# A gated-feature attention stage: another order of its round, TensorE's blocks in two pieces, two feature turns copied by VectorE

## What is computed

```python
def _psi(x):                                  # x: tokens x 64 of one head
    gen = x @ proj_w.T + proj_b
    A, Bg, Th = gen[..., 0:8], gen[..., 8:16], clip(gen[..., 16:24], -8, 8)
    return concat([A * exp(Th) + Bg * cos(Th), Bg * sin(Th)])
Q = Q_input @ Wq_w.T + Wq_b                   # K and V are the context itself
pq, pk = _psi(Q), _psi(K)
tensor, spinor = <two bilinear forms of pq and pk>
wedge = sqrt(max(|pq|^2 |pk|^2 - tensor**2 - spinor**2, 0) + 1e-6)
hodge = sqrt(|pq|^2 + 1e-6) * sqrt(|pk|^2 + 1e-6)
w = softmax((g0*wedge + g1*tensor + g2*spinor + g3*hodge) / 4 / temperature)
out = (w @ V) @ Wo_w.T + Wo_b
x = layernorm(x + out)
```

## Time and profile before

| | |
|---|---|
| runs of the kernel before | 2824.83, 2836.79, 2835.43 us |
| the profiled execution: its own time, its span | 2834.78 us, 2833.1 us |
| busy in the span: PE, PEld | 2371.9 us (84%), 1503.3 us (53%) |
| busy in the span: DVE, ACT, POOL | 1695.8 us (60%), 1363.7 us (48%), 325.7 us (11%) |
| mean granted TensorE clock | 0.908 of full speed |
| the psi stage, first transposes to last norm | 2006.9 to 2580.5 us of the span |

### The profile page before, as it was taken

How to read it: one execution, slowest core, us unless ns; L and a number is a source line. 1 busy time by engine, 2 the same in 40 slices (tenths; PEclk the granted TensorE clock), 3 DMA queues, 4 the chain that set the end, 5 groups by cost and what they waited for, 6 DMA issues and landing times. The chain is left out here.

```text
span 2833.1 us, 32030 instructions
## 1 busy us (share of the span) xinstructions
PE 2371.9 (84%) x11624; PEld 1503.3 (53%) x11624; DVE 1695.8 (60%) x3500; ACT 1363.7 (48%) x1968; POOL 325.7 (11%) x299
## 2 busy tenths in 40 slices
PE   6888888876888888887999699997568878777998
PEld 4656666652333333334566456565355655555886
DVE  5666666624666666654643598989566666743232
ACT  2333333311555555562222565654188888782221
POOL 0000000000000000000156400000111111100000
PEclk7999999966999999999899899998789999998999
DMA  2000000006333333214034512111200000002000
GB/s 77 8 16 15 16 16 15 8 8 165 53 68 68 61 66 57 47 27 162 16 59 65 106 38 68 45 68 46 102 8 31 30 31 30 23 15 75 15 23 23
DMA packets 104949, 132.46 MB, mean 47 GB/s; under 512 B 21748, under 2 KB 87556, under 8 KB 104792
## 3 DMA queue, kind: packets, MB, share of 16 engines
q1 hardware_dynamic: 90440, 115.58, 15.2%
q0 software_dynamic: 11904, 14.69, 3.2%
q10 hardware_dynamic: 2448, 0.14, 0.1%
HBM read 73.69 MB, written 31.20 MB: 37 GB/s over the span
## 5 line engine op out<-in xcount | busy, mean ns | idle before, releaser
L987 DVE TENSOR_REDUCE xattn_tops<-region 128x2 f32<-128x1024 f32 x256 | 306.3, 1220 | 128.9 <-PE region L771 128.8
L924 ACT ACTIVATE xattn_probs<-region 128x1024 f32<-128x1024 f32 x256 | 256.3, 1022 | 126.1 <-PE region L760 125.0
L156 PE MATMUL region<-gla_xT,weights_even 128*128 128x512 f32 (+1 forms) x416 | 200.6, 637 | 21.0 <-ACT gla_xT L248 21.0
L760 PE MATMUL region<-xattn_qs,xattn_ks 49*128 49x512 f32 x512 | 126.6, 496 | 61.8 <-DVE xattn_tops L987 31.4
L156 PE MATMUL region<-mamba_xT,weights_odd 128*128 128x512 f32 x320 | 156.4, 636 | 3.1 <-DVE mamba_xh L1988 3.1
L2491 DVE CUSTOM_DVE_ANT_0 weights_even<-psi_wedge,region,psi_unsign 128x512 f32<-128x512 f32 x128 | 95.4, 746 | 98.9 <-ACT psi_wedge L2325 97.3
L156 PEld LDWEIGHTS region<-gla_xT,weights_even 128*128 128x128 f32 (+1 forms) x416 | 77.1, 192 | 133.9 <-issue 107.0
L789 PE MATMUL region<-xattn_probs,xattn_va 128*32 128x512 f32 x1024 | 142.6, 624 | 1.4 <-ACT xattn_o_T L951 1.4
L771 PE MATMUL region<-xattn_ks,xattn_qs 48*128 48x512 f32 x512 | 126.5, 493 | 13.0 <-DMA xattn_ks<-xattn_khi 8.6
L165 PE MATMUL region<-weights_even,gla_work 128*128 128x256 f32 x512 | 119.6, 394 | 17.6 <-DVE gla_work L631 11.0
L760 PEld LDWEIGHTS region<-xattn_qs,xattn_ks 49*128 49x128 f32 x512 | 48.9, 190 | 141.0 <-DVE xattn_tops L987 70.8
(11 more groups left out here) (534 smaller groups left out, 5377.4 us busy)
## 6 DMA issues: line engine op xcount, KB each, us to landing
weights_even<-mamba_cs SPq DMA_DIRECT2D x32, 512.0 KB, 4.7
xattn_qs<-xattn_qhi SPq DMA_DIRECT2D x128, 64.0 KB, 2.3
xattn_ks<-xattn_khi SPq DMA_DIRECT2D x128, 64.0 KB, 2.3
moe_sums<-moe_picked SPq DMA_DIRECT2D x9, 512.0 KB, 7.8
gla_x<-in_x SPq DMA_DIRECT2D x8, 512.0 KB, 3.8
x_after_gla<-gla_res SPq DMA_DIRECT2D x8, 512.0 KB, 2.9
xattn_x<-x_after_gla SPq DMA_DIRECT2D x8, 512.0 KB, 4.1
xattn_ctxT<-in_ctxT SPq DMA_DIRECT2D x8, 512.0 KB, 4.4
```

The lines of the kernel that those rows point to most:

```text
L156: last = st.nc.tensor.matmul(o[0:m, i, :], w[:, c, col + i * P:col + i * P + m], rhs[:, c, :], start=c == 0, stop=c == kc - 1)
L760: last = mm(o[:, r, :], ks[rows, ring(n), a, j * P:j * P + P], qs[rows, ring(n), a, :], start=True, stop=True)
L924: A_(probs[:, p % 3, a, :, :], st.region(f"k{v}")[:], ACT.Exp).then_inc(st.emptying(f"k{v}"), 1)
L987: V.tensor_reduce(tops[:, n % 2, t, a::2], st.region(f"q{u}")[:], AX, ALU.max).then_inc(st.emptying(f"q{u}"), 1)
```

## The change

The round's list is written in another order. `Q`, `gen`, `pv` and `out` are each cut into two pieces (`pv` by key blocks, so that a piece needs two turns only), and one score tile stands between the pieces of a block; `pv` of heads 0 and 1 moves from behind the next round's score 0 to the end of its own round, and `out` from behind score 15 to between scores 13 and 15. `recip` becomes a piece of its own ahead of `features` 0, and `sums` moves to behind score 1. `split` 0 is cut in two, which makes three parts, and the last part moves to behind `angles` 2. The copies of feature turns 1 and 2 go from ScalarE to VectorE. No arithmetic changes.

The order's table, two lines of the many that move (what they do is shown below):

```diff
                 yield "score", b, 13
+                yield "out", b - 1, 0
+                yield "split", b + 1, 1
                 yield "angles", b + 2, 1
...
+                yield "fT", b + 1, 1
+                yield "turn", b, 0
                 yield "norm", b - 1, 0
```

The pieces on TensorE (`Q` alike: one matmul pair to each piece):

```diff
                     elif what == "gen":
...
+                        if i == 0:
+                            pe.wait_ge(st.sem("ctxT_in"), 16 * (b + 1))
...
+                            st.claim(f"gen{b}")
+                        else:
+                            pe.wait_ge(*st.emptied(f"Q{b}"))
+                        o, a, src = st.region(f"gen{b}"), 1 - i, QT if i else ctxT
...
                     elif what == "pv":
+                        c, part = divmod(i, 2)
...
+                        for h in (2 * c, 2 * c + 1):
+                            pe.wait_ge(*st.emptied(f"pT{b}_{h}_{part}"))
+                        o = st.region(f"pv{b}_{c}") if part else st.claim(f"pv{b}_{c}", ring="pv")
+                        for j in (2 * part, 2 * part + 1):
...
                     elif what == "out":
+                        if i == 0:
+                            for c in range(DC):
+                                pe.wait_ge(*st.emptied(f"pv{b}_{c}"))
+                            st.claim(f"out{b}")
+                        o = flat(st.region(f"out{b}")[:])
+                        for t in (2 * i, 2 * i + 1):
```

The copies, off ScalarE and on VectorE:

```diff
-                    elif what == "fT":
+                    elif what == "fT" and i not in (1, 2):
                         act.wait_ge(*st.full(f"fT{b}_{i}"))
...
+                    elif what == "fT" and i in (1, 2):
+                        dve.wait_ge(*st.full(f"fT{b}_{i}"))
...
+                        if i == 1:
+                            V.tensor_copy(fL[0:64, 0, :], o[0:64, 0, :])
+                            V.tensor_copy(fL[64:P, 1, :], o[64:P, 0, :])
+                            last = V.tensor_copy(fQ[:, 0, :], o[:, 1, :])
+                        else:
+                            V.tensor_copy(fK[0:64, 0::2, :], o[0:64, :, :])
+                            last = V.tensor_copy(fK[64:P, 1::2, :], o[64:P, :, :])
+                        last.then_inc(st.emptying(f"fT{b}_{i}"), 1)
```

More of the change, by code:

```diff
@@ L2110, in order @@
                 yield "score", b, 13
+                yield "out", b - 1, 0
+                yield "split", b + 1, 1
                 yield "angles", b + 2, 1
                 yield "score", b, 14
+                yield "out", b - 1, 1
                 yield "angles", b + 2, 2
+                yield "split", b + 1, 2
                 yield "score", b, 15
@@ L2145, in _ @@
                     elif what == "Q":
[L2146 to L2149, removed]
-                    elif what == "gen":
[L2151 to L2160, removed]
-                        last.then_inc(st.filling(f"gen{b}"), 1)
+                        if i == 0:
+                            pe.wait_ge(*st.emptied(f"xT{b}"))
+                            if b == 0:
+                                weights.arrive(pe)
+                            st.claim(f"Q{b}")
@@ L2226, in _ @@
                     elif what == "out":
-                        for c in range(DC):
-                            pe.wait_ge(*st.emptied(f"pv{b}_{c}"))
-                        token_major(st, f"out{b}", featT, wo)
+                        if i == 0:
+                            for c in range(DC):
+                                pe.wait_ge(*st.emptied(f"pv{b}_{c}"))
+                            st.claim(f"out{b}")
+                        o = flat(st.region(f"out{b}")[:])
+                        for t in (2 * i, 2 * i + 1):
+                            for c in range(DC):
+                                last = mm(o[:, t * D:t * D + D], featT[:, c, t * P:t * P + P], wo[:, c, :],
+                                          start=c == 0, stop=c == DC - 1)
+                        if i:
+                            last.then_inc(st.filling(f"out{b}"), 1)
             @block.sync
@@ L2286, in _ @@
                         A_(featT[:], st.region(f"xT{b}")[:], ACT.Copy).then_inc(st.emptying(f"xT{b}"), 1)
-                    elif what == "Q":
+                    elif what == "Q" and i == DC - 1:
                         act.wait_ge(*st.full(f"Q{b}"))
@@ L2431, in split_of @@
                         V.tensor_copy(q_high, q_wide)
-                        step(V.tensor_copy(tK[:], feat[:, kg, 0:64].unsqueeze(2).to_broadcast([P, GQ, 2, 64])))
+                        V.tensor_copy(tK[:], feat[:, kg, 0:64].unsqueeze(2).to_broadcast([P, GQ, 2, 64])).then_inc(
+                            st.sem("high"), 1)
+                    elif i == 1:
+                        dve.wait_ge(st.sem("high"), b + 1)
                         TT(q_low, q_wide, q_high.bitcast(F32), ALU.subtract)
```

88 lines of the change are left out of this document (49 added, 39 removed).

## The result

Four executions of the changed kernel gave 2905.53, 2928.97, 2896.99 and 2916.51 us, median 2911.02; beside a median of 2832.85 for the kernel before that is a ratio of 1.0283 (95% interval 1.0218 to 1.0348): slower, by 78 us, where 2873 and a range up to 2894 had been forecast.

The account below looks back on a forecast made before the run. ScalarE was taken as nearest to the bound, busy 53.98 of a 64.83 us round. Full rounds +35, round 6 +5, round 0 -3, entry +2, exit -1: 38 us on 2834.78, so 2873 us, range 2844 to 2894.

Parts of the forecast that it names:

- the junction: From ScalarE's table load for the exponentials to the next batch's score 0; 20.71 us before, to grow by 2.7 to 6.0.
- S: Point where ScalarE begins score 0 of the next batch; forecast 23.4 to 26.7 us behind X, where it was 20.71.
- X: Point where ScalarE begins the exponentials, its table load; the score stretch from S to it took 44.12 us.
- the chain as written: Junction steps in series: residual 3.9 to 4.6 us, feature turns 2.0 to 3.6, VectorE's copies and norm 13.6, end 3.9 to 4.9.
- the pieces: Eight pieces of Q, pv, gen and out between scores 8 and 15: about 1.05 us ScalarE wait each, 8.5 in all.
- the front of the stretch: From score 0 on: ScalarE waits about 2 us, plus 1 to 3 at score 2, spread and feature turn 4; 3 to 5.
- the pieces lose the clock: Rival: all eight pieces at 3.73 us for 2.00, TensorE needing 14 us more a round; 2945 us; chance 0.04.
- The order: Score 0 to the exponentials: 11.5 to 13.5 us of ScalarE waits for 9.8, growth 1.7 to 3.7, taken 2.5.
- Five full rounds: Rounds with both junction and score stretch, each to grow by 7 us (4.4 to 9.7): 35 (22 to 48).
- Round 6: Keeps the junction's loss without the features' pieces: 5 us more (3 to 6).
- Round 0: No residual or norm, so feature turn 0 doesn't wait and ScalarE's saving shows: -3 us.
- Entry: Start of the stage: the last part of split waits behind gen and angles, +2 us (0 to 4).

Follow-up runs that it names:

- e1: The changed kernel with the copies of feature turns 1 and 2 back on ScalarE; 2914.05 us in one run, rounds 78.4 us for 79.0.
- e2: The changed kernel with the norm moved behind the fourth copy of the probabilities' turns on VectorE; 2891.06 us in one run.
- e4: The changed kernel with both pieces of the output projection moved back behind exp 0, uncut; 2892.73 us in one run.
- e7: The changed kernel with the two pieces of Q, gen, pv of heads 2 and 3 and out back to back; 2895.98 us in one run.
- e14: e9 with everything from score 6 to the exponentials' table load in the order of the kernel before, blocks whole; 2808.94 us, ratio 0.9936 to the kernel before.
- e9: The changed kernel with late norm, uncut projection behind exp 0, old front order, recip ahead of features 0, features 1 and 2 later; 2838.70 us, ratio 1.003.
- e6: The changed kernel with TensorE's idle places filled by 96 spare transposes more a round; 2869.64 us in one run, rounds 73.0 us for 79.0.
- e11: The kernel before with 30 spare transposes on TensorE between score 2 and sums; 2831.99 us, ratio 1.0003.
- e10: e9 with 22 spare transposes on TensorE between score 2 and sums; 2820.45 us, ratio 0.9979 to the kernel before.
- e5: The changed kernel with the front of its round, score 0 to features 4, in the order of the kernel before; 2890.86 us in one run.

## Why the prediction was right or wrong

**Right: direction and the junction.** It was put at 2.7 to 6.0 us more, 4.5 taken; measured 5.75 (26.7 less 21.0), which is S at 26.4 to 27.1 us behind X, the top of the 23.4 to 26.7, by the chain as written: residual ends 4.6 us behind X, turns 0 and 1 at the lower clock, norm, fourth copy, a 7.3 us wait of ScalarE. e1, e2 and e4 take its links out one by one. Casts cost 0.69 and 1.21, for 0.62 and 1.16.

**Right in size: the pieces.** "8.5 us for eight" was ScalarE's wait at the scores 8 to 15; 8.3 were measured behind score 8 and 1.07 at it. The working was less good than the number: by the earlier trace rows a piece takes 1.8 to 2.0 us, not "1.5 to 1.9", so that 1.8 and 0.98 less 1.4 would have made 11 for eight. e7 shows that the cut itself moves the stretch by 0.4 us at most. The middle's new order is not free: with the old middle, blocks whole, e14's stretch is 1.6 us shorter than e9's.

**Wrong: the front of the stretch, which was priced without the lower clock.** The step that failed is the term of "3 to 5" us for new waits "at the front": it measured 6.7 and 11.3. It named the places, score 2, `spread` and feature turn 4, and the idle time, but gave the lower clock behind it no price. TensorE idled 3.11 and 2.31 us ahead of score 2 and the fifth turn, because `sums` takes a region of the ring and the claims then wait for tails 0 and 1, and then ran at 0.50. "In this part of the round TensorE would have hardly an idle us" was said of the pieces, which do run at 1.00; it did not hold for the front. e6 gives the price: of the 13.6 us by which the mean round grew, filling removes 6.1, 4.0 in the stretch and 2.1 in the junction; 7.6 stay. The Trainium skill (Perfetto Trace Analysis, Matmul Optimizations) asks for matmuls in back-to-back batches; I had set that rule aside, and e6 bears it out in kind, e11 and e10 do not in size. The rival "the pieces lose the clock" had the cause in the wrong place and at twice the size: 14 us a round, for 6.1.

**The order, a little under its size.** With hardly any low clock left (e6) the stretch is still 3.9 us longer than before, where 2.5 (1.7 to 3.7) was taken: 1.9 ahead of score 8 and 2.0 behind it. ScalarE's waits in e6's stretch come to 13.9 us (47.97 less 34.12), just above the 11.5 to 13.5 of the forecast. So the forecast's +7 a round is near the 7.6 that stay with TensorE kept busy, in part by luck: its 4.5 for the junction had the lower clock in it, and e6 has 3.7 there. e5, with the old front, is 3.6 us shorter than the changed kernel, but its clock differs too.

**Sizes around it.** Five full rounds: 68 us for 35. Round 6 grew by 8.3 for 5. Round 0 grew by 1.7 for -3: its junction did fall by 2.2, its stretch, left out of the term, grew by 3.9. Entry +3.0 for +2. "Exit -1" forgot the stretch of round 7, 5.4 us longer: +6.4.

**Signs.** `sums` came 75.6 and 81.2 us apart, not 70 to 74; ScalarE's wait ahead of feature turn 3 (7.3), VectorE's ahead of the casts (3.8) and of tail 0 (5.4 to 5.9) and ScalarE's 1 us at the scores 9 to 15 were as named.

Open: why the clock falls behind the first idle place in one round and behind the second in the next, its share in e1's uneven junctions, and how the order and the clock divide e5's gain. No run here settles these.

## What to carry to other kernels

Price a new order with the clock at both levels: list every place where a claim or a copy makes TensorE idle (3.11 and 2.31 us here), and ask which blocks run behind it. Cutting blocks moved the stretch by 0.4 us at most by itself (e7); what counted in the junction was which instructions stood ahead of the one copy that the next stage needs. Try a change's parts alone: the part that gains (here copies off the bound engine, with the norm out of the way) can hide behind the parts that lose.

## What the runs showed of the hardware that was not expected

A VectorE instruction stood still while GpSimd added. From the timelines of VectorE and GpSimd in the kernel after:

```profile
2280.24 2.93 DVE L2432 TENSOR_TENSOR psi_feat<-psi_prods 128x896 f32<-128x896 f32 x1
...
2287.08 1.09 DVE L2436 TENSOR_TENSOR psi_feat<-psi_prods 128x896 f32<-128x896 f32 x1
...
2279.84 2.38 POOL L2581 TENSOR_TENSOR psi_x<-psi_x,rows 128x1024 f32<-128x1024 f32 x1 [6.91 <-PE region L148]
```

Two instructions of one size: 1.09 us alone, 2.93 beside the add, and the slow one ends 0.95 us behind the add's end (2283.17 and 2282.22). In the other kind of round it is 1.86 us, again ending 0.95 behind the add. The Trainium skill (GPSIMD Engine Reference, Specifications) says that VectorE instructions with two SBUF inputs contend with GpSimd; the trace agrees. Which of the two waits goes by which began first, as e14 shows:

```profile
2248.25 1.09 DVE L2432 TENSOR_TENSOR psi_feat<-psi_prods 128x896 f32<-128x896 f32 x1
2249.38 2.76 DVE L2405 TENSOR_TENSOR psi_prods<-psi_z 128x512 f32<-128x512 f32 x1
...
2248.68 2.91 POOL L2581 TENSOR_TENSOR psi_x<-psi_x,rows 128x1024 f32<-128x1024 f32 x1
```

The first began 0.43 us ahead of the add and kept its 1.09 us, and the add took 2.91 for 2.38; the second, 0.69 us by itself, began inside the add, took 2.76 and ended 0.55 behind it. In the kernel after, the order had brought L2432 and the add together in the full rounds. Its 0.8 to 1.8 us more lie ahead of tail 5, for which TensorE waits 3.20 us in the timeline above, but what they cost a round was not tried alone: e14 has 2.07 us of the kind and the stretch of the kernel before.

Spare transposes can shorten a round (e6, 73.0 us for 79.0), and can also only move the low clock to the next block (e11).
